# Gather indices read straight from the lists, and one signal per fold step, in a graph network kernel

## What is computed

```python
h = relu(layernorm(x));  x = x + sage(h, src, dst)        # three layers with a max pool over the edges
h = relu(layernorm(x));  x = x + attention(h, src, dst)   # 8 heads, softmax over the edges of a node

# sage: pool(h)[v] = max of h[src] over the edges with dst == v, 0 where there is none
h1 = relu(h @ Wp1.T + bp1);            p1 = pool(h1)
y  = relu([h, p1] @ Wm1.T + bm1);      p2 = pool(y)
z  = layernorm(relu([y, p2] @ Wm2.T + bm2) + y);  p3 = pool(z)
out = layernorm(relu([z, p3] @ Wm3.T + bm3) + z)

# attention: q, k, v = linear(h); per edge e of row r (rows = src, cols = dst)
s = <q[r], k[c]> per head;  a = softmax of s over the edges of r;  out[r] = sum a * v[c];  out @ Wo + bo
```

## Time and profile before

| | us |
|---|---|
| median of three runs | 5759.88 |
| the profiled execution | 5784.07 |
| its span, first to last instruction | 5782.3 |
| POOL busy | 3624.6 (63%) |
| DVE busy | 3373.5 (58%) |
| PE busy | 1135.6 (20%) |
| ACT busy | 429.5 (7%) |

### The profile page before, as it was taken

The page is one execution under the profiler, slowest core; times in us unless marked ns, Lnnn a source line. Parts: engine busy times, 40 slices in busy tenths (PEclk is TensorE's granted clock), DMA queues, the critical chain, the costliest instruction groups (busy, mean ns, idle before and its releaser), DMA issues. The chain is left out here.

```text
span 5782.3 us, 24077 instructions
## 1 busy us (share of the span) xinstructions
PE 1135.6 (20%) x4114; PEld 729.4 (13%) x4114; DVE 3373.5 (58%) x7030; ACT 429.5 (7%) x1091; POOL 3624.6 (63%) x3767
## 2 busy tenths in 40 slices
PE   3333311116223201061222000185000000000005
PEld 3222211114111100041111000153000000000003
DVE  4666666654444443363455333375777777777776
ACT  3000000002000000030000000042000000000001
POOL 1676666746666676646767766523766666666653
PEclk9555555558555555585555555597555555555557
DMA  4555555535555555555556555535656666666653
GB/s 131 174 190 181 185 179 190 192 128 167 190 198 188 199 196 186 188 176 190 194 195 206 197 180 184 168 122 162 201 169 189 187 189 187 188 190 189 189 173 102
DMA packets 341065, 1039.46 MB, mean 180 GB/s; under 512 B 73625, under 2 KB 140966, under 8 KB 307504
## 3 DMA queue, kind: packets, MB, share of 16 engines
q0 software_dynamic: 209536, 613.51, 36.1%
q1 hardware_dynamic: 131376, 424.41, 19.9%
HBM read 649.96 MB, written 388.08 MB: 180 GB/s over the span
## 5 line engine op out<-in xcount | busy, mean ns | idle before, releaser
L473 POOL DMA_INDIRECT G<-tab,ix x2349 | 2297.6, 978 | 1001.7 <-issue 687.1
L503 DVE SCALAR_TENSOR_TENSOR G<-G,reset 128x256 f32<-128x256 f32 x2349 | 1065.2, 479 | 1485.3 <-DMA G<-tab,ix 737.3
L1448 POOL DMA_INDIRECT kv<-kvtab,ix x936 | 884.4, 945 | 285.0 <-issue 285.0
L1446 POOL DMA_INDIRECT q<-qtab,ix x234 | 221.0, 945 | 415.6 <-remote 192.8
L1564 PE MATMUL trio<-ident,state 128*128 128x128 f32 x6 | 1.9, 426 | 1681.7 <-DVEq L1586 1681.7
L595 PE MATMUL tail<-ident,h 128*128 128x128 f32 x294 | 94.0, 421 | 1184.2 <-DVE U L564 471.6
L1468 DVE TENSOR_TENSOR kv<-kv,wide 128x3072 f32<-128x3072 f32 x78 | 260.8, 3344 | 26.9 <-issue 21.3
L1470 DVE TENSOR_REDUCE s<-kv 128x96 f32<-128x3072 f32 x78 | 261.5, 3353 | 2.7
L860 PE MATMUL trio<-hot 128*128 128x196 bf16 x783 | 143.0, 366 | 541.6 <-DVE hot L839 243.2
L1275 POOL DMA_INDIRECT pool<-hist,nix x147 | 139.3, 948 | 121.6 <-DVE nix L1281 70.8
L1564 PEld LDWEIGHTS trio<-ident,state 128*128 128x128 f32 x6 | 1.2, 219 | 1682.5 <-DVEq L1586 1682.5
(11 more groups left out here) (323 smaller groups left out, 3603.7 us busy)
## 6 DMA issues: line engine op xcount, KB each, us to landing
hist<-G SPq DMA_DIRECT2D x261, 1152.0 KB
G<-tab,ix POOLq DMA_INDIRECT x2349
ahist<-state SPq DMA_DIRECT2D x78, 408.0 KB
tab<-o SPq DMA_DIRECT2D x147, 128.0 KB
kv<-kvtab,ix POOLq DMA_INDIRECT x936
h<-tab SPq DMA_DIRECT2D x98, 128.0 KB
G<-tab SPq DMA_DIRECT2D x98, 128.0 KB
kvtab<-okv SPq DMA_DIRECT2D x49, 256.0 KB
```

Source lines behind the costliest of these rows:

```text
L473: g.indirect_dma_start(G[b][:, k, :], None, tab, bass.IndirectOffsetOnAxis(ix[:, b, k:k + 1], 0)).then_inc(s_eg[b].sem, 16)
L503: ins = v.scalar_tensor_tensor(out=G[b][:, k, :], in0=before, scalar=reset[:, at:at + 1], in1=G[b][:, k, :], op0=ALU.add, op1=ALU.max)
L1446: g.indirect_dma_start(qs[b][:, r, :], None, qtab, bass.IndirectOffsetOnAxis(ix[:, b, R * SLOT + r:R * SLOT + r + 1], 0)).then_inc(s_query ...
L1448: g.indirect_dma_start(kvs[b][:, k, :], None, kvtab, bass.IndirectOffsetOnAxis(ix[:, b, k:k + 1], 0)).then_inc(s_eg[b].sem, 16)
```

## The change

The tile `ix`, its copies (`place`) and the semaphore `c_eix` go. A gather takes its index column straight from `src_ix`, `dst_ix` or `row_node`. A new count `c_taken` tells POOL when a buffer may be written again: in a max pass fold 2 signals it, in the attention pass the addition `pairs`. Of the nine folds only fold 2 (`c_taken`), fold 5 (`chain`) and fold 8 (`c_batch`) signal, and only folds 0, 3 and 6 wait, each for the last fold of the step before. In the attention pass the query gathers of a batch wait for ACT's copy of three batches before, and only the key and value gathers wait for `c_taken`.

```diff
@@ max_pass, POOL
-                        g.wait_ge(c_eix.sem, c_eix.of(i, b, UB))
+                        if i * UB + b >= 2:
+                            g.wait_ge(c_taken.sem, c_taken.of(i, b - 2, UB))
                         g.wait_ge(s_hs[b].sem, s_hs[b].base + i * 16)
                         for k in range(J):
-                            g.indirect_dma_start(G[b][:, k, :], None, tab, bass.IndirectOffsetOnAxis(ix[:, b, k:k + 1], 0)).then_inc(s_eg[b].sem, 16)
+                            at = edge(i * UB + b, k)
+                            g.indirect_dma_start(G[b][:, k, :], None, tab, bass.IndirectOffsetOnAxis(src_ix[:, at:at + 1], 0)).then_inc(s_eg[b].sem, 16)
@@ max_pass, DVE
-                    def place(b, n):
...
                             if k == 0:
                                 v.wait_ge(s_eg[b].sem, s_eg[b].base + (i * (16 * J) + 16 * J))
-                            if k == C - 1 and n:
-                                v.wait_ge(c_batch.sem, c_batch.of(i, b - 1, UB))
-                            elif j or n:
-                                v.wait_ge(chain.sem, done[k - C if j else k - C + J])
+                                if n:
+                                    v.wait_ge(c_batch.sem, c_batch.of(i, b - 1, UB))
+                            elif k == C:
+                                v.wait_ge(c_taken.sem, c_taken.of(i, b, UB))
+                            elif k == 2 * C:
+                                v.wait_ge(chain.sem, done[0])
...
                             if k == J - 1:
                                 ins.then_inc(c_batch.sem, 1)
-                            else:
-                                done[k] = chain.inc(ins)
-                            if k == 2 * C - 1:
-                                place((b + 2) % UB, n + 2)
+                            elif k == C - 1:
+                                ins.then_inc(c_taken.sem, 1)
+                            elif k == 2 * C - 1:
+                                done[0] = chain.inc(ins)
@@ attention_pass, POOL
-                        g.wait_ge(c_eix.sem, c_eix.base + times(i, b, 2))
+                        n = i * UB + b
+                        if i:
+                            g.wait_ge(c_query, times(i - 1, b, 1))
                         for r in range(R):
-                            g.indirect_dma_start(qs[b][:, r, :], None, qtab, bass.IndirectOffsetOnAxis(ix[:, b, R * SLOT + r:R * SLOT + r + 1], 0)).then_inc(s_query[b], 16)
+                            at = r * NBA + n
+                            g.indirect_dma_start(qs[b][:, r, :], None, qtab, bass.IndirectOffsetOnAxis(row_node[:, at:at + 1], 0)).then_inc(s_query[b], 16)
+                        if i:
+                            g.wait_ge(c_taken.sem, c_taken.of(i - 1, b, UB))
                         for k in range(R * SLOT):
-                            g.indirect_dma_start(kvs[b][:, k, :], None, kvtab, bass.IndirectOffsetOnAxis(ix[:, b, k:k + 1], 0)).then_inc(s_eg[b].sem, 16)
+                            at = (k % R * NBA + n) * SLOT + k // R
+                            g.indirect_dma_start(kvs[b][:, k, :], None, kvtab, bass.IndirectOffsetOnAxis(dst_ix[:, at:at + 1], 0)).then_inc(s_eg[b].sem, 16)
@@ attention_pass, DVE
-                        chain.inc(v.tensor_tensor(pairs[:, :, :, :].rearrange("p a r f -> p (a r) f"), first, vals[:, HALF:2 * HALF, :], ALU.add))
+                        v.tensor_tensor(pairs[:, :, :, :].rearrange("p a r f -> p (a r) f"), first, vals[:, HALF:2 * HALF, :], ALU.add).then_inc(c_taken.sem, 1)
                         chain.link(v.tensor_tensor(state[b][:, :, D:ACC], held[:, :, D:ACC], z_row[:, :, :], ALU.add))
-                        place(b, i * UB + b + UB)
+                        v.wait_ge(c_taken.sem, c_taken.of(i, b, UB))
```

More of the change, by code:

```diff
@@ L169, in gnn_kernel @@
         eps = sb(top, "eps", [P, 1])
-        ix = sb(top, "ix", [P, UB, R * SLOT + R], I32)
         nix = sb(top, "nix", [P, UN], I32)
@@ L201, in gnn_kernel @@
         s_hs = [Count(sem(f"s_hs{b}")) for b in range(UB)]
-        c_eix, c_batch, c_w, c_e = (Count(sem(n)) for n in ("c_eix", "c_batch", "c_w", "c_e"))
+        c_taken, c_batch, c_w, c_e = (Count(sem(n)) for n in ("c_taken", "c_batch", "c_w", "c_e"))
         s_held = {"vector": sem("s_held_v"), "pool": sem("s_held_p")}
@@ L461, in max_pass, with edge @@
         def max_pass(G, side, tiles, marks=None):
+            def edge(n, k):
+                return k % C * (CH // C) + n * STEPS + k // C
             with block() as blk:
@@ L489, in _ @@
                     side.start(v)
-                    done = [0] * J
+                    done = [0]
                     def fold(k):
@@ L496, in stage @@
                                 v.wait_ge(s_eg[b].sem, s_eg[b].base + (i * (16 * J) + 16 * J))
[L497 to L500 removed]
+                                if n:
[4 more added lines that the diff above has]
+                                v.wait_ge(chain.sem, done[0])
                             before = G[b][:, k - C, :] if j else G[(b - 1) % UB][:, J - C + c, :]
[L502 removed]
+                            at = edge(n, k)
                             ins = v.scalar_tensor_tensor(out=G[b][:, k, :], in0=before, scalar=reset[:, at:at + 1],
@@ L539, in _ @@
                     staged(a, NB, UB, fill + side.scalar(a, evac))
-            c_eix.close(NB)
+            c_taken.close(NB)
             c_batch.close(NB)
@@ L1452, in _ @@
                 def _(v):
-                    def place(b, n):
-                        if n < NBA:
-                            v.tensor_copy(ix[:, b, 0:R * SLOT].rearrange("p (e r) -> p r e", r=R), of_slot[:, :, n, :]).then_inc(c_eix.sem, 1)
-                            v.tensor_copy(ix[:, b, R * SLOT:R * SLOT + R], of_row[:, :, n]).then_inc(c_eix.sem, 1)
                     chain.link(v.memset(state[UB - 1][:, :, :], 0.0))
-                    for m in range(UB):
-                        place(m, m)
                     def score(i, b):
@@ L1523, in _ @@
                         sp.wait_ge(s_hs[b].sem, s_hs[b].base + (NBA // UB) * 16)
-            c_eix.close(2 * NBA)
+            c_taken.close(NBA)
             c_batch.close(NBA)
```

## The result

The changed kernel takes 5823.2 us (median; 5793.0 to 5836.9) where the kernel before, run beside it, takes 5757.8 us (5755.3 to 5779.2): ratio 1.010, 95% interval 1.0068 to 1.0133. It is slower by 1%; the forecast was 5404 us, the range 5320 to 5610. The profiled execution has a span of 5817.2 us (5782.3 before).

The account below looks back on a forecast made before the run. The prediction took POOL to bound the max passes. It took 240 us there and 116 in attention, 356 in all, off the profiled 5784.07 (5428), less 24 for the median of the runs: 5404 us, range 5320 to 5610.

Parts of the forecast that it names:

- POOL bounds the passes, and its waits are all that can be won: Max passes: gathers cost POOL 3012 of 3318 us; only its waits beyond the ordinary, 278 us, can be won.
- Earlier release, -126 to -202 us: Max passes: gathers released by fold 2 instead of fold 5 and the copy; 1 to 2 us given back per wait.
- prediction's own last sign: The sum fails if the late signals follow the gathers and not DVE's own signals; no size given.
- 4.9 us of waiting turn into 1: First max pass, one stall: POOL's 4.9 us wait becomes about 1 us of waiting for the store.
- Fewer signals, together with the release 240 us: Max passes: six of nine fold waits disappear, returning up to 76 to 152 us; 240 us for both parts.
- rival A: Signals cost nothing, only the release moves: 5584 us, chance 0.16; its sign, folds 0, 3 and 6 wait 3 us each.
- A wait costs 1.05 us: Slow stretches of the max passes: each fold waits 1.05 us, so nine folds take 7.5 us in place of 13.8.
- Copies and L1497 in attention, -116: Attention pass: 12 us from the dropped copies and 104 us from L1497's shorter wait; bounds 12 and 171.
- the reading of the wait: Attention: L1497 waits because L1496's signal is queued behind those of two copies; 2.04 us per batch falls to 0.7.
- the lists as indices cost nothing: All 3519 gathers: index columns straight from a list change nothing; bounds -0.003 and +0.06 us each.
- C: Rival: without pauses POOL keeps DVE's signals late all the time, 336 us more in the passes, 5980 us; chance 0.04.

Follow-up runs that it names:

- i_before_late_pe: The kernel before, with the product of every sixth node tile in pass 1 (9 of 49) done ten times before its signal: 5770.1 us, ratio 1.001.
- i_after_late_pe: The changed kernel, with the product of every sixth node tile in pass 1 (9 of 49) done ten times before its signal: 5850.5 us, ratio 1.0148.
- e2_thin_only: The kernel before, copies and release kept, only folds 2, 5 and 8 signal and only folds 0, 3 and 6 wait: 5794.8 us, ratio 1.0011.
- h_before: The kernel before itself, unchanged, run for its trace in a set without late signals: ratio 1.0001.
- e1_release_only: The changed kernel, but all nine folds signal and wait as in the kernel before: 5832.1 us, ratio 1.0065.

## Why the prediction was wrong, step by step

**POOL bounds the passes, and its waits are all that can be won: right.** Where no signal is late, POOL has no such wait, and the passes of the changed kernel take 1017 + 1003 + 1025 = 3045 us, the 3012 of the gathers plus the ends.

**Earlier release, -126 to -202 us: the step that failed.** It was meant to shorten the passes; with it they are 74 us longer in the profile (80 with all folds signalling). In rows 4 the step held the start of the addition, 334.28, fixed and let POOL go on at 330.57. But the rows had the tie in them: POOL stopped at 335.45 - 5.18 = 330.27, and the late signal came 4.0 us after that. The prediction's own last sign, late signals that follow the gathers and not DVE's own signals, is what came. Take the stop away and the signal moves with it, as i_before_late_pe and i_after_late_pe show; "4.9 us of waiting turn into 1" became 14.60. The step was right that the store is what POOL waits for next, but that store stands behind the stall itself.

**Fewer signals, together with the release 240 us: nothing.** e2_thin_only has 1.0011. The sign of rival A is what the trace shows: in the third pass folds run in groups of three, and each group waits about 3 us:

```profile
3402.49 1.33 DVE L502 SCALAR_TENSOR_TENSOR G<-G,reset 128x256 f32<-128x256 f32 x3 [3.55 <-issue]
3406.69 1.28 DVE L502 SCALAR_TENSOR_TENSOR G<-G,reset 128x256 f32<-128x256 f32 x3 [2.87 <-remote]
3410.26 1.28 DVE L502 SCALAR_TENSOR_TENSOR G<-G,reset 128x256 f32<-128x256 f32 x3 [2.29 <-remote]
```

From 3390 to 3502 us 81 folds wait 78.9 us, 0.97 each, where 73 waited 76.6. "A wait costs 1.05 us" was the wrong unit: a batch waits some 9 us in both kernels, whether in three waits or in nine. The Trainium skill ("VectorE: DVE Perf Modes", "The DRAIN you can't avoid"), by which a semaphore costs nothing extra, agrees with the 1.0011 of e2_thin_only, and rows 6 were misread against it.

**Copies and L1497 in attention, -116: -23 to -33.** The gain is there, at a fifth to a quarter of its size. The wait fell from 159.1 us to 79, -80 for the forecast's -104. But it came back elsewhere. DVE groups of the attention pass, kernel before, then after:

```profile
L1486 DVE TENSOR_TENSOR trio<-kv,wide 128x1536 f32<-128x1536 f32 x77 | 135.6, 1761 | 77.2 <-issue 76.8 <-ACT wide L1513 0.3
L1493 DVE TENSOR_TENSOR pairs<-trio,kv 128x1536 f32<-128x1536 f32 x77 | 135.3, 1757 | 88.0 <-DVE tail L1491 69.3 <-issue 15.5 <-remote 3.1
L1496 DVE TENSOR_TENSOR tail<-tail,pairs 128x768 f32<-128x768 f32 x77 | 73.7, 957 | 0.3 <-DVE state L1494 0.3
```

```profile
L1485 DVE TENSOR_TENSOR trio<-kv,wide 128x1536 f32<-128x1536 f32 x77 | 135.8, 1763 | 98.0 <-issue 98.0
L1492 DVE TENSOR_TENSOR pairs<-trio,kv 128x1536 f32<-128x1536 f32 x77 | 135.4, 1758 | 106.0 <-DVE tail L1490 105.7
L1495 DVE TENSOR_TENSOR tail<-tail,pairs 128x768 f32<-128x768 f32 x76 | 73.5, 967 | 18.1 <-issue 17.8
L1496 DVE TENSOR_TENSOR state<-tail,pairs 128x768 f32<-128x768 f32 x76 | 72.8, 958 | 78.5 <-issue 39.5 <-DVE tail L1495 38.8
```

Three other waits grew by 20.8 + 18.0 + 17.8 = 57 us. Nor was the reading of the wait right, that L1496's signal stands in a queue behind those of the two copies: in h_before the copies are there and L1497 waits 2.7 us in all.

```profile
L1497 DVE TENSOR_TENSOR state<-tail,pairs 128x768 f32<-128x768 f32 x78 | 74.7, 957 | 2.7
```

POOL waits no more for indices, yet its gathers stretch: 1031 and 1079 ns where they were 945. They are 945 in both kernels without late signals, so the lists as indices cost nothing; that step was right (980 for 978 ns in the passes). What stretches them is open; no run tells whether a gather waits there or is slow.

**The rivals.** C named the mechanism, POOL without pauses keeping signals late, and had a chance of 0.04. It priced it as folds of three passes, 336 us; it sat in TensorE's signal in the first pass, 62 us. It was set aside because three waits a batch would have to be 3.2 us each; what decided was how far POOL runs on while DVE stands.

**What no step considered**: that the lateness is not part of the kernel. 344 of the forecast's 356 us (all but the copies) were priced from waits that are there in one condition only. The forecast of 5404 us would have been nearer where signals are prompt (5305.7 us), for a reason that the change has no part in: there the kernel before takes 5313 to 5323.

**What stays open.** What puts a chip into the one or the other condition (the granted clock is 0.56 to 0.57 in both). By what path POOL's gathers, or their transfers, hold a signal back, and why some signals come through all the same; the runs made for it (product first, pause, half rows) all fell in the prompt condition. Whether pass 1 without tile work escapes the loss in late condition: the three runs of it all fell in the other. No version was faster in both conditions: attention alone is faster than the kernel before with late signals (5763.8 us, 0.9955) and 0.9998 without; the changed kernel is 0.9971 without and 1.010 with them.

## What to carry to other kernels

Before a late signal in a trace is taken as fixed, look what the busiest issuing engine did just before it came: here signals that mostly arrived some microseconds after POOL's last gather moved when that gather moved. A release that lets an engine run further ahead of a stalled one helps only if the stall ends by itself. And a trace of before should be taken in more than one session before its waits are priced: nearly 8% of this kernel's time was gone when the same kernel ran on the same chip at another time, 35 minutes apart.

## What the hardware showed that was not expected

- The same kernel on the same chip (number 12 on record) took 5323.0 us (16 runs) and 35 minutes later 5762.2 us (13 runs), each set steady within 1%. The medians of the kernel before were 5757.8 us beside the result, and 5794.5, 5316.8, 5323.0, 5313.5 and 5762.2 us in the five sets.
- In the late condition a signal of TensorE reached DVE up to 27 us after its matmul, and in 10 of the 11 long waits in pass 1 of e1_release_only 3.3 to 6.3 us after POOL's last gather; in 5 of the 12 of the changed kernel it came while POOL was issuing.
- Back-to-back gathers of 128 rows start 1.25 us apart, with 1024 or 512 bytes a row, and with a memset of 0.12 us between them.
